# Layer 1's transposes by rows in a third PSUM bank, with the copy of layer 0's first outputs moved to the start of layer 1

## The reference, cut to what matters

```
x = x + L0_xattn(layernorm(x), ctx)    # 16 heads of 64, softmax over 375 context rows, @ Wo + bo
x = x + L0_ffn(layernorm(x))           # quantised linear, depthwise convolution, silu, linear
x = x + L1_xattn(layernorm(x), ctx)    # 16 heads of 16, rms norm and rope on q and k
x = x + L1_ffn(layernorm(x))           # quantised with one scale over all batches
```

## Time and profile before

| what | value |
|---|---|
| median of 3 runs | 2360.57 us (2360.05 to 2366.0) |
| the profiled execution's own time | 2361.02 us |
| its span, first to last instruction | 2359.2 us |
| PE busy | 2286.8 us (97%) |
| DVE, POOL, ACT busy | 1743.7 (74%), 1691.7 (72%), 1587.5 us (67%) |
| mean granted TensorE clock | 0.995 |

### The profile page before, as it was taken

One profiled execution on the slowest core, in us unless ns is written; L12 is line 12 of the kernel. 1 busy time (PEld: TensorE's weight loads), 2 busy tenths in 40 slices (PEclk: granted clock), 3 DMA queues, 4 the chain that ended last, 5 costly groups with the idle time before them and its releaser, 6 DMA issues.

```text
span 2359.2 us, 62966 instructions
## 1 busy us (share of the span) xinstructions
PE 2286.8 (97%) x20874; PEld 1830.5 (78%) x20874; DVE 1743.7 (74%) x4342; ACT 1587.5 (67%) x4467; POOL 1691.7 (72%) x1863
## 2 busy tenths in 40 slices
PE   7999999999999999999999999999999999999788
PEld 6778877778788777778877778787777878877546
DVE  5777777787777777777777777777778777778785
ACT  6666666776667677666766766666677666667356
POOL 2777777777777777777787777777777777877607
PEclk9999999999999999999999999999999999999899
DMA  4000000000000000000000000000000000001202
GB/s 147 10 11 10 10 8 10 2 10 10 10 10 9 10 2 10 10 10 10 10 8 9 4 10 10 10 10 8 10 2 10 10 10 10 8 4 36 57 11 63
DMA packets 31472, 37.06 MB, mean 16 GB/s; under 512 B 3301, under 2 KB 29653, under 8 KB 31445
## 3 DMA queue, kind: packets, MB, share of 16 engines
q1 hardware_dynamic: 31444, 36.71, 5.3%
HBM read 29.36 MB, written 7.34 MB: 16 GB/s over the span
## 4 chain that ended last, share of the span: by engine, by line
PE 88%; DVE 4%; ACT 4%; issue 3%; POOL 2%; DMA 0%; POOLq 0%; ACTq 0%; SPq 0%; DVEq 0%
PE ps L367 25%; PE pt L471 11%; PE ps L447 10%; PE pa L483 7%; PE pt L461 5%; PE ps L411 5%; PE pa L523 4%; PE pa L498 4%; ACT probT L828 3%; PE ps L435 2%; PE pa L367 2%; PE pt L367 2%; PE pa L633 1%; PE ps L426 1%; DVE th L1547 1%
## 5 line engine op out<-in xcount | busy, mean ns | idle before, releaser
L1145 DVE TENSOR_REDUCE nmx<-ps 112x2 f32<-112x750 f32 x512 | 478.2, 934 | 142.2 <-PE ps L447 91.4
L1643 POOL TENSOR_TENSOR prob<-prob,rinv 112x375 f32<-112x375 f32 x512 | 404.2, 810 | 130.3 <-DVE rinv L1153 130.2
L1643 POOL TENSOR_TENSOR prob_last<-prob_last,rinv 112x375 f32<-112x375 f32 x512 | 411.9, 830 | 59.1 <-DVE rinv L1153 59.0
L828 ACT ACTIVATE room<-ps 128x376 f32<-128x376 f32 (+2 forms) x480 | 227.5, 487 | 265.9 <-PE ps L367 265.9
L828 ACT ACTIVATE probT<-pt 125x336 f32<-125x336 f32 (+1 forms) x512 | 242.6, 474 | 167.8 <-PE pt L461 112.5
L868 ACT ACTIVATE prob<-ps,nmx 112x375 f32<-112x375 f32 x512 | 289.9, 581 | 65.0 <-DVE nmx L1145 65.0
L868 ACT ACTIVATE prob_last<-ps,nmx 112x375 f32<-112x375 f32 x512 | 290.7, 584 | 8.2 <-DVE nmx L1145 8.2
L1670 POOL TENSOR_TENSOR krs<-krs,nhalf 125x48 f32<-125x48 f32 x32 | 257.0, 8030 | 0.0
L1136 DVE COPY probT<-pt 125x336 f32<-125x336 f32 x322 | 161.9, 503 | 97.4 <-PE pt L471 97.3
L483 PE MATMUL pa<-probT,room 125*64 125x112 f32 x3072 | 183.0, 265 | 0.0
L471 PEld LDWEIGHTS pt<-ident,prob 112*125 112x125 f32 x966 | 118.5, 189 | 72.7 <-issue 64.2
(11 more groups left out here) (294 smaller groups left out, 5981.0 us busy)
## 6 DMA issues: line engine op xcount, KB each, us to landing
craw<-in_ctx SPq DMA_DIRECT2D x32, 375.0 KB, 3.1
xin<-in_x SPq DMA_DIRECT2D x32, 112.0 KB, 2.0
x_rows<-x SPq DMA_DIRECT2D x32, 112.0 KB, 1.9
out<-probT SPq DMA_DIRECT2D x16, 224.0 KB, 2.3
room<-x_rows SPq DMA_DIRECT2D x1, 2576.0 KB, 13.7
w<-in_f1w SPq DMA_DIRECT2D x2, 1024.0 KB, 6.6
stage<-in_wk SPq DMA_DIRECT2D x2, 512.0 KB, 4.7
stage<-in_wv SPq DMA_DIRECT2D x1, 1024.0 KB, 7.5
```

The lines of the kernel that those rows point to most:

```text
L828: return act.activation(dst, src, ACT.Copy)
L1145: top = dve.tensor_reduce(nmx[:, g:g + 2], ps[0:T, 2 * (i % 2):2 * (i % 2) + 2, 0:S], AX_X, ALU.max, negate=True)
L1643: pool.tensor_tensor(prob(i, n), prob(i, n), rinv[:, g:g + 1].to_broadcast([T, S]), ALU.mult).then_inc(s["normed"], 1)
```

## The change

Three things are changed.

1. The by-rows transposes of pairs 7, 9 and 11 (`third_room`; 1 and 3 in the CLOSING attention) put their lower 48 rows in pa bank 0 and not in pt bank 1. So the whole turn that follows (pairs 8, 10, 12; 2 and 4 in CLOSING) puts its head 0 in pt bank 1 (`whole_bank`), which is free, and its head 1 in pt bank 0, for which it waits on ACT's copy of the upper rows.
2. pa bank 0 must be read before that: ACT copies it to `oT` at the end of its step 5, behind `exps(7)` (before: step 14), and DVE writes `oT_lo` in its step 6, behind `turned(5)` (before: behind step 15). `turn(7)`, `turn(9)` and `turn(11)` wait for it (`o_lo`). Layer 1's output copy gets a semaphore of its own (`o1_sb`).
3. DVE's `query_rest` stands in step 10, behind `turned(9)`, and not in step 5, behind `turned(4)`.

```diff
+        def third_room(i, part):
+
+            first = LEAD + 2 if part == MIDDLE else 0
+            return part != OPENING and by_rows(i, part) and first < i < first + PAIRS - 2
+
+        pt_upper = pt[0:SK, 0, 0:2 * KT * 64]
+
+        def pt_lower(i, part):
+
+            return (pa[0:SK, 0, :] if third_room(i, part) else pt[0:SK, 1, :])[:, 0:2 * KT * (T - 64)]
+
+        def whole_bank(i, n, part):
+
+            return 1 - n if third_room(i - 1, part) else n
...
             def turn(i, part, b):
 
+                if part == MIDDLE and third_room(i, part):
+                    pe.wait_ge(s["o_lo"], b * 2 + 3)
                 if by_rows(i, part):
                     pe.wait_ge(s["pT_even"], at(i, part, b))
                     pe.wait_ge(s["pT_odd"], at(i, part, b))
...
-                    if part != OPENING or i >= 1:
-                        pe.wait_ge(s["pT_odd" if n else "pT_even"], at(i, part, b))
+                    if third_room(i - 1, part):
+                        pe.wait_ge(s["pT_even"], at(i - 1 + n, part, b))
+                        pe.wait_ge(s["pT_odd"], at(i - 1, part, b))
+                    elif part != OPENING or i >= 1:
+                        pe.wait_ge(s["pT_odd" if n != whole_bank(i - 1, 0, part) else "pT_even"], at(i, part, b))
...
-                    if part != CLOSING and i == count - 2:
-                        act.wait_ge(s["pv"], at(count - HT, part, b))
-                        copy(oT[:, 0:HT, :], pa[:, 0, 0:HT * T].rearrange("p (j t) -> p j t", j=HT))\
-                            .then_inc(s["o_sb"], 1)
+                    if part == OPENING and i == count - 2:
+                        o0_copy(at(HT, part, b))
...
+                        if part == MIDDLE and i == 5:
+                            o0_copy(at(HT, part, b))
...
-                    if part == MIDDLE and i == 5:
+                    if part == MIDDLE and i == 10:
                         query_rest(b)
+                    if part == MIDDLE and i == 6:
+                        values_lo(k, 0)
                 if part == OPENING:
                     dve.wait_ge(s["w_quant"], 2)
                 if part != CLOSING:
-                    values_lo(k, 0)
+                    if part == OPENING:
+                        values_lo(k, 0)
                     k1_squares(k, 0)
```

More of the change, by code:

```diff
@@ L238, in xattn_ffn_kernel @@
             "x_in ctx_in cT_hi cT_lo k0_ready k0_sb v0_ready v0_sb var0 rstd0 xn0_ready xT0_ready xT0_sb "
-            "q0_ready q0_sb k0_hi k0_lo k1_hi k1_lo hp_zero xbo_ready scores maxed exped recip normed pT pT_even pT_odd pv o_sb o_lo wo_ready x1_ready "
+            "q0_ready q0_sb k0_hi k0_lo k1_hi k1_lo hp_zero xbo_ready scores maxed exped recip normed pT pT_even pT_odd pv o_sb o1_sb o_lo wo_ready x1_ready "
             "var1 rstd1 xq_ready diag_ready xqT_ready rb_ready xqT_sb rb_sb kv1_ready kv1_sb h_ready h_sb conv0 "
@@ L460, in turn @@
                                 col = (n * KT + t) * (e - r)
-                                last = pe.transpose(pt[0:SK, bank, col:col + e - r],
+                                last = pe.transpose((pt_upper, pt_lower(i, part))[bank][:, col:col + e - r],
                                                     prob(i, n)[r:e, t * SK:(t + 1) * SK], ident[r:e, r:e])
@@ L467, in turn @@
                     pe.wait_ge(s["normed"], 2 * at(i, part, b) + n + 1)
-                    if part != OPENING or i >= 1:
-                        pe.wait_ge(s["pT_odd" if n else "pT_even"], at(i, part, b))
+                    if third_room(i - 1, part):
[3 more added lines that the diff above has]
+                        pe.wait_ge(s["pT_odd" if n != whole_bank(i - 1, 0, part) else "pT_even"], at(i, part, b))
                     for t in range(KT):
-                        last = pe.transpose(pt[0:SK, n, t * T:(t + 1) * T],
+                        last = pe.transpose(pt[0:SK, whole_bank(i, n, part), t * T:(t + 1) * T],
                                             prob(i, n)[:, t * SK:(t + 1) * SK], ident[0:T, 0:T])
@@ L508, in wo1_product @@
             def wo1_product(b):
-                pe.wait_ge(s["o_sb"], b * 3 + 3)
+                pe.wait_ge(s["o1_sb"], b + 1)
                 for c in range(DC):
@@ L514, in wo0_product @@
             def wo0_product(b, half):
-                pe.wait_ge(s["o_sb"], b * 3 + (half + 1))
+                pe.wait_ge(s["o_sb"], b * 2 + (half + 1))
                 if half == 0:
@@ L857, in turned @@
                     act.wait_ge(s["pT"], 2 * at(i, part, b) + 1)
-                    copy(probT[:, 2 * (i % 4), :, :], pt[0:SK, 0, 0:KT * T].rearrange("p (k t) -> p k t", k=KT))\
+                    copy(probT[:, 2 * (i % 4), :, :], pt[0:SK, whole_bank(i, 0, part), 0:KT * T].rearrange("p (k t) -> p k t", k=KT))\
                         .then_inc(s["pT_even"], 1)
@@ L936, in query_copies, with o0_copy @@
                 ins.then_inc(s["q1_sb_act"], 1)
+            def o0_copy(done):
+                act.wait_ge(s["pv"], done)
+                copy(oT[:, 0:HT, :], pa[:, 0, 0:HT * T].rearrange("p (j t) -> p j t", j=HT)).then_inc(s["o_sb"], 1)
             def o1_copy(part, b):
                 act.wait_ge(s["pv"], at(PAIRS + (LEAD if part == MIDDLE else 0), part, b))
-                copy(oT1[:], pa[:, 1, 0:DC * T].rearrange("p (j t) -> p j t", j=DC)).then_inc(s["o_sb"], 1)
+                copy(oT1[:], pa[:, 1, 0:DC * T].rearrange("p (j t) -> p j t", j=DC)).then_inc(s["o1_sb"], 1)
             def rest(b, last_batch):
@@ L1132, in turned @@
                     dve.tensor_copy(probT[:, 2 * (i % 4):2 * (i % 4) + 2, :, 64:T],
-                                    pt[0:SK, 1, 0:2 * KT * (T - 64)].rearrange("p (n k t) -> p n k t", n=2, k=KT))\
+                                    pt_lower(i, part).rearrange("p (n k t) -> p n k t", n=2, k=KT))\
                         .then_inc(s["pT_odd"], 1)
@@ L1136, in turned @@
                     dve.tensor_copy(probT[:, 2 * (i % 4) + 1, :, :],
-                                    pt[0:SK, 1, 0:KT * T].rearrange("p (k t) -> p k t", k=KT))\
+                                    pt[0:SK, whole_bank(i, 1, part), 0:KT * T].rearrange("p (k t) -> p k t", k=KT))\
                         .then_inc(s["pT_odd"], 1)
@@ L1198, in values_lo @@
             def values_lo(b, half):
-                dve.wait_ge(s["o_sb"], b * 3 + (half + 1))
+                dve.wait_ge(s["o_sb"], b * 2 + (half + 1))
                 part = slice(HT * half, HT * half + HT)
```

## The result

The changed kernel takes 2485.9 us (median of 4 runs, 2479.07 to 2488.62). The kernel before, with one more run beside it, takes 2362.78 us (median of 4 runs). The ratio is 1.0518, with a 95% interval from 1.0503 to 1.0533: slower by 5.2%, 123 us, where 28 us had been forecast.

What follows compares the result with a forecast made beforehand. PE's stream was taken to set the time. A pass summed +0.12 - 0.40 + 1.98 - 0.38 - 0.39 = +0.93 us, times 31 +28.8, CLOSING -0.8: +28.0 us, forecast 2389 us, range 2372 to 2401 (8 in 10).

Steps and rivals of the forecast that it cites:

- That is worth -0.40, -0.38, -0.39 us: At turn(8), turn(10) and turn(12): the third bank removes PE's three stalls behind scores, 0.40, 0.38 and 0.39 us a pass.
- I take +0.12 us: In DVE's step 6: oT_lo delays pair 9's largest values and so scores(11), +0.12 us a pass, between 0 and 0.4.
- I take 1.98: At scores(13): PE stands 1.98 us a pass, waiting for q's rest behind DVE's copy of turn(9); bounds 1.59 and 2.94.
- the rule's estimate of 1.0 us: For q's rest: it waits until POOL's first division ends, then runs some 0.4 us; a stall of 2.05 us at scores(13).
- Behind scores(13) nothing is late in turn: After the stand: scores(15) is not delayed, and turn(13)'s second head waits at most 0.2 us.
- third rival: Late scores delay divisions or copies, or oT_lo and q's rest cost more: 9 to 30 us each, 2398 to 2420; 12 in 100.
- The clock: Rival: a 2 us stand each pass lowers the granted clock, 2.5 us more a pass, 31 times, 78 us: 2466; 2 in 100.
- The faster rival: At scores(13): q's rest is there in time, no stall, -1.05 us a pass: 2328 us; 4 in 100.

Runs made afterwards that it cites:

- e1: The changed kernel with q's rest put back in step 5, so the third bank and early oT copy stand alone: 2358.95 us, ratio 0.9991.
- e5: The changed kernel with q's rest in step 9 and the banks of turn(13) (turn(5) in CLOSING) exchanged: 2346.04 us, ratio 0.9937.
- e4: The changed kernel with q's rest in step 9, without the exchange of banks at turn(13): 2356.12 us, ratio 0.9979.
- e3: The changed kernel with eight matmuls whose results nobody reads put in front of scores(13): 2414.13 us, ratio 1.0232.
- e2: The kernel before with only q's rest moved from step 5 to step 10: 2483.24 us, ratio 1.0519.
- e6: The changed kernel with q's rest still in step 10, but ahead of the copy of turn 9: 2390.6 us, ratio 1.0132.

## Why the prediction was wrong

The direction was right, and the size was not: +123 us against +28 us, far outside the range.

- **"That is worth -0.40, -0.38, -0.39 us"** (the stalls removed): mis-sized. The 0.61 us on which it rested is the time of scores ahead of a by-rows turn. Ahead of a whole turn it stays longer: scores(11) to turn(8) went from 1.01 to 0.74 us (1049.93 to 1050.67), scores(13) to turn(10) from 0.99 to 0.69 us (620.88 to 621.57), scores(15) to turn(12) from 1.00 to 0.79 us (624.30 to 625.09), and each such turn itself takes 0.84 instead of 0.81 us. The gain is 0.27 + 0.30 + 0.21 - 0.09 = 0.69 us, not 1.17. Why 0.1 to 0.2 us stay was not tested.
- **"I take +0.12 us"** for oT_lo in step 6: within its bounds. Turn(7), up to the start of scores(11), took about 0.05 us more (0.62 us in the changed kernel, 1049.31 to 1049.93; 0.58 before), and scores(11) was not late beyond that.
- **"I take 1.98"** (the stand at scores(13)): right. turn(9) to scores(13) took 2.53 us (1052.95 to 1055.48) instead of 0.59, 1.94 us more. q_lo took 0.98 us, which is the rule's estimate of 1.0 us rather than the 0.93 us of the row.
- **"Behind scores(13) nothing is late in turn ... turn(13)'s second head would wait at most 0.2 us"**: wrong, and for a reason that the text did not look at. turn(13) started 0.43 us late (1.15 instead of 0.72 us behind the products, by the starts above and the earlier trace rows), with an idle time ended by DVE's copy of turn(12). The exchange of banks that frees turn(12) makes turn(13)'s first head wait for the copy that comes last. e1 shows it without any stand, and e5 against e4 shows what the banks are worth: 10 us. The diff had it: where a bank is handed over in other order, the next user's wait is part of the change.
- **The sum of these** is -0.69 + 0.05 + 1.94 + 0.43 = +1.73 us a pass, 54 us for 31: that is e3, 2414.13 us. The forecast had 0.93 us a pass, 29 us. The missed 25 us would by themselves have put the time outside the range. 2414 us lies in the third rival's 2398 to 2420 us, but not by its causes: oT_lo cost 0.05 us, q's rest waited out one division and not both, and what made turn(13) late was its bank.
- **The clock**, priced at 78 us with 2 chances in 100: the step that failed. It was argued away with a stretch in which PE was busy for 11.10 of 15 us at full clock. e2 and e3 show that a stand of 1.94 us, once a pass, in a stream that is otherwise full, does make the granted clock fall in most passes; e6's profiled execution shows none of it at 1.1 us. The price was near: 70 us in all against the rival's 78, but in 27 passes of unequal falls and not 2.5 us in each of 31. The stretch at 2185 to 2200 us was lower in its busy share, but its single stands were shorter; the longest idle time in it is 1.55 us, against 1.66 at scores(13):

```profile
2190.55 0.27 PE L610 MATMUL pt<-identb,xq 112*128 112x112 bf16 x2 [1.55 <-DVE xq L1218]
```

Whether these 0.1 us, or what PE did around the stands, made the difference is left open.

- **The faster rival** is out as argued: nothing here hid a wait for an instruction that itself waits for the instruction ahead (31 stands in 31 passes).

## What to carry to other kernels

A wait can't be hidden where what it waits for itself waits for the last instruction of the engine that waits: when an instruction is moved "later but still ahead of its use", follow the wait back through the engine it is moved to. On a TensorE that is busy nearly all the time, a new stand can cost twice, by its length and by the granted clock behind it: price both, and test the second with matmuls that nobody reads. When buffers change hands in a new order, look at the next user of the buffer that is now emptied last: that wait is where a removed stall comes back (e1: no gain; with the next pair's banks exchanged and q's rest in a gap of DVE, e5: 0.6% faster).

## What the runs showed of the hardware that was not expected

- A single stand of PE of 1.94 us in a pass of some 70 us made the granted clock fall in 27 of 31 passes of the changed kernel and in 23 of 31 of e2, with a mean of 0.96 from 200 to 2100 us in both, and some 70 us of time. With eight idle matmuls in the stand the clock was 1.00; with three (about 1.2 us of unbroken stand left) it fell in 3 of 31; with a stand of 1.1 us in none, each read from the one execution that was profiled.
- It did not fall in every pass: behind the stand that ended at 620.88 us it stayed at 1.00, behind the one that ended at 1055.48 us it was 0.58 over 3.4 us.
- The same VectorE instruction of two SBUF inputs took 0.49 us begun ahead of GpSimd's division (e6), and 0.98, 0.93 or 0.89 us begun 0.19 us (the changed kernel), 0.24 us or 0.28 us (e5, division at 1065.73) behind it.
